# Turning the first expert loop's rows by transposing transfers, with gathers three tiles ahead

## The reference

```python
out = jnp.einsum('teh,te->th', y, combine)           # layer 0: routed experts
sh = jax.nn.gelu(x_flat @ sW1 + sb1, approximate=False)
out = out + sh @ sW2 + sb2                           # and the shared one
...
h = jax.nn.gelu(x_flat @ W1e + b1e, approximate=False)   # layer 1, per expert
y = h @ W2e + b2e
out = acc + ce[:, None] * y
```

## Time and profile before

| | us |
|---|---|
| median of 3 runs | 786.86 (783.21 to 787.51) |
| the profiled execution | 785.51 |
| its span, first to last instruction | 783.7 |
| PE busy | 672.7 (86%) |
| DVE busy | 494.1 (63%) |
| ACT busy | 462.3 (59%) |
| POOL busy | 312.5 (40%) |

### The profile page before, as it was taken

One profiled execution on the slowest core, in us unless ns is written; L12 is line 12 of the kernel. 1 busy time (PEld: TensorE's weight loads), 2 busy tenths in 40 slices (PEclk: granted clock), 3 DMA queues, 4 the chain that ended last, 5 costly groups with the idle time before them and its releaser, 6 DMA issues.

```text
span 783.7 us, 21835 instructions
## 1 busy us (share of the span) xinstructions
PE 672.7 (86%) x7498; PEld 592.1 (76%) x7499; DVE 494.1 (63%) x1227; ACT 462.3 (59%) x1124; POOL 312.5 (40%) x229
## 2 busy tenths in 40 slices
PE   4787899988987899999999936872399999999993
PEld 3454566768877899999989935762399999999993
DVE  4569758696857676777755525967288644544541
ACT  2346667875638786777755615250198766666661
POOL 1100014343562454556555422243235554454442
PEclk9879879999999999999999976955599999999997
DMA  8860100012619633678863339835534454444541
GB/s 263 289 206 28 54 1 1 28 54 71 201 42 317 180 49 53 152 223 246 238 169 46 48 72 409 290 107 116 195 55 79 79 81 72 81 73 68 80 67 22
DMA packets 84451, 96.19 MB, mean 123 GB/s; under 512 B 27419, under 2 KB 70181, under 8 KB 83638
## 3 DMA queue, kind: packets, MB, share of 16 engines
q1 hardware_dynamic: 69334, 74.81, 29.6%
q0 software_dynamic: 15072, 20.84, 16.9%
HBM read 63.73 MB, written 26.79 MB: 115 GB/s over the span
## 4 chain that ended last, share of the span: by engine, by line
PE 66%; DVE 14%; DMA 7%; ACT 4%; issue 4%; POOL 2%; SPq 1%; POOLq 0%; ACTq 0%; DVEq 0%
PE bank L1153 8%; PE bank L1151 8%; PE bank L1152 8%; PE bank L1164 7%; PE bank L1165 7%; PE bank L1166 7%; DMA x_arena<-token_rows,gather_now 3%; DVE weights L1597 2%; DVE ln_stats L1924 2%; PE bank L872 1%; DMA x_sum<-x_arena,add_now 1%; POOL weights L727 1%; PE bank L1043 1%; DVE weights L1691 1%; PE bank L874 1%
## 5 line engine op out<-in xcount | busy, mean ns | idle before, releaser
L1448 ACT ACTIVATE work<-bank,b_cols 128x128 f32<-128x128 f32 x624 | 178.1, 382 | 155.8 <-PE bank L1153 153.0
L1151 PE MATMUL bank<-x_arena,weights 128*128 128x128 f16 x1248 | 217.0, 221 | 11.3 <-DMA x_arena<-x_arena 10.6
L1152 PE MATMUL bank<-x_arena,weights 128*128 128x128 f16 x1248 | 216.9, 221 | 0.0
L1153 PE MATMUL bank<-x_arena,weights 128*128 128x128 f16 x1248 | 216.8, 221 | 0.0
L1849 DVE TENSOR_TENSOR work<-work 128x512 f16<-128x512 f32 x156 | 100.9, 688 | 138.8 <-ACT work L1456 119.4
L1164 PE MATMUL bank<-weights,work 128*128 x624 | 170.1, 273 | 0.0
L1166 PE MATMUL bank<-weights,work 128*128 x624 | 170.1, 273 | 0.0
L1165 PE MATMUL bank<-weights,work 128*128 x624 | 170.1, 273 | 0.0
L1151 PEld LDWEIGHTS bank<-x_arena,weights 128*128 x1248 | 123.5, 99 | 12.2 <-DMA x_arena<-x_arena 10.7
L1152 PEld LDWEIGHTS bank<-x_arena,weights 128*128 x1248 | 123.5, 99 | 0.4
L1153 PEld LDWEIGHTS bank<-x_arena,weights 128*128 x1248 | 123.6, 99 | 0.0
(11 more groups left out here) (214 smaller groups left out, 1207.1 us busy)
## 6 DMA issues: line engine op xcount, KB each, us to landing
weights<-in_L_ffn_W SPq DMA_DIRECT2D x76, 256.0 KB, 7.0
raw<-in_L_ffn_W SPq DMA_DIRECT2D x44, 256.0 KB
split_dram<-row_arena SPq DMA_DIRECT2D x12, 512.0 KB
weights<-split_dram SPq DMA_DIRECT2D x3, 2048.0 KB, 16.7
token_rows<-row_arena SPq DMA_DIRECT2D x2, 2072.0 KB, 10.8
x_arena<-in_x SPq DMA_DIRECT2D x4, 512.0 KB, 6.5
weights<-in_L_ffn_sW SPq DMA_DIRECT2D x8, 256.0 KB, 7.3
x_sum<-x_arena SPq DMA_DIRECT2D x4, 512.0 KB, 3.2
```

The lines of the kernel that those rows point to most:

```text
L1151: nc.tensor.matmul(o, w1_at[f][c][0].block(), hi, start=c == 0, stop=False)
L1152: nc.tensor.matmul(o, w1_at[f][c][0].block(), lo, start=False, stop=False)
L1153: m = nc.tensor.matmul(o, w1_at[f][c][1].block(), hi, start=False, stop=c == DC - 1)
L1448: m = nc.scalar.activation(hid[:, k, f * P:f * P + P], h_ps[k][half][:, g * P:g * P + P], ACT.Gelu, bias=b1_cols[n][:, f, bass.ds(e, 1)], ...
```

## The change

SyncE turns layer 0's rows too, with the same transposing transfer, so `xT_in` gets a semaphore per layer, and TensorE's turns, their PSUM banks and VectorE's copies go. SyncE's list is written anew: units 28..31 as soon as the table of rows is stored, units 24..27 once TensorE has read the router's scratch (`table_done` in place of `routed`; `padding` moves out of that scratch), turn(0, 0), the store of x batch 3, turn(0, 1), `biases`, units 32..35 and two units of layer 1, and then one turn for each tile 2 to 38, with at most one unit of layer 1 loaded and one staged between two turns. The late loads for layer 1 stand behind turn 33. Gathers go out three tiles ahead in both loops: gather 0 before the last shared_low, gathers 1 and 2 ahead of the loop, gather j+3 in body j. VectorE's pick now waits for the transfer.

```diff
-            for b in range(2, B):
-                store_x(0, b, s_added, TB * (b + 1))
-            biases(0)
-            sp.wait_ge(routed, 1)
-            for u in range(24, 28):
-                load_unit(0, u)
+            store_x(0, 2, s_added, 3 * TB)
             sp.wait_ge(rows_stored[0], 16)
             for u in range(28, 32):
                 load_unit(0, u)
+            sp.wait_ge(table_done, 1)
+            for u in range(24, 28):
+                load_unit(0, u)
+            sp.wait_ge(x_stored[0][0], 16)
+            turn(0, 0)
+            store_x(0, 3, s_added, 4 * TB)
+            sp.wait_ge(x_stored[0][1], 16)
+            turn(0, 1)
+            biases(0)
             sp.wait_ge(s_down_done, STEPS)
             for u in range(32, 36):
                 load_unit(0, u)
...
+            for j in range(2, ROUTED):
+                turn(0, j)
+                if j == PRESPLIT_FROM + AHEAD_UNITS[1] + 5:
+                    late_loads()
+                u = j - PRESPLIT_FROM - 3
+                if 0 <= u < AHEAD_UNITS[1]:
+                    split_done(sp, 1, u)
+                    if u + RAW < AHEAD_UNITS[1]:
+                        load_unit(1, u + RAW)
+                    if u >= KEPT:
+                        stage(u)
...
+            def turn(n, j):
+
+                k = j % 2
+                sp.wait_ge(row_in[k][n], 16 * (j // 2 + 1))
+                if j >= 2:
+                    sp.wait_ge(up_done[n], 2 * (j - 1))
+                sp.dma_start_transpose(xT[:, k, :].rearrange("p (i r) -> p i r", r=P), rows_in[:, k, 0:2 * D]).then_inc(xT_in[k][n], 16)
...
-                    if before_end(j, 2):
-                        gather(n, j + 2, k)
+                    if before_end(j, 3):
+                        gather(n, j + 3, 1 - k)
...
+                gather(n, 1, 1)
+                gather(n, 2, 0)
                 tile_loop(pool, n, body)
...
                 def up(j, q, k):
-                    if n == 0:
-                        pe.wait_ge(xT_ready, j + 1)
-                    else:
-                        pe.wait_ge(xT_in[k], 16 * (q + 1))
+                    pe.wait_ge(xT_in[k][n], 16 * (q + 1))
...
-                    if n == 0 and before_end(j, 1):
-                        turn(j + 1, q + (1 if k else 0), 1 - k)
                     up(j, q, k)
...
-                def pick_weight(j, k):
-
+                def pick_weight(j, q, k):
+
+                    dve.wait_ge(xT_in[k][n], 16 * (q + 1))
```

More of the change, by code:

```diff
@@ L214, in build @@
         from_tile = [w[:, 0:TT * (ROUTED + 1)].bitcast(F16).rearrange("p (k t i) -> p k t i", k=2, t=TT) for w in scratch]
-        padding = [w[:, 0:ROUTED + 1] for w in scratch]
+        padding = r_b[:, 0:ROUTED + 1]
         tile_hot = [w[:, 704:704 + TT * (ROUTED + 1)].bitcast(F16).rearrange("p (k t i) -> p k t i", k=2, t=TT) for w in scratch]
@@ L260, in build @@
         few_ps = bank[7][:, 0:FC * 32].rearrange("p (f r) -> p f r", f=FC)
-        xT_ps = [bank[k][:, 0:256].bitcast(F16) for k in range(2)]
         h_ps = [bank[2:4], bank[4:6]]
@@ L330, in build @@
         row_in = [per_layer(f"row_in{k}") for k in range(2)]
-        rowT_done, xT_ready = sem("rowT_done"), sem("xT_ready")
-        xT_in = [sem(f"xT_in{k}") for k in range(2)]
+        xT_in = [per_layer(f"xT_in{k}") for k in range(2)]
         up_done, hi_done = per_layer("up_done"), per_layer("hi_done")
@@ L647, in _, with late_loads @@
                 load_unit(1, u)
[L648 to L661, removed]
+            def late_loads():
+                for k in range(4):
+                    sp.wait_ge(staged[k], 16 * 3)
+                sp.wait_ge(kvm_stored, 32)
+                sp.wait_ge(kvb_stored, 16)
+                sp.dma_start(kvm.rearrange("p b c e -> p (b c e)"), kv_dram).then_inc(late_in, 16)
+                sp.dma_start(kvb.rearrange("p b d -> p (b d)"), kv_bias_dram).then_inc(late_in, 16)
+                sp.dma_start(gamma, a["L1_xattn_ln_gamma"].partition_broadcast(P)).then_inc(late_in, 16)
+                sp.dma_start(beta, a["L1_xattn_ln_beta"].partition_broadcast(P)).then_inc(late_in, 16)
+            for j in range(2, ROUTED):
[9 more added lines that the diff above has]
+                        stage(u)
             sp.wait_ge(added[0], 16 * ROUTED)
@@ L680, in _ @@
                 load_unit(1, u)
[L682 to L688, removed]
             for b in range(2):
@@ L692, in _ @@
             for j in range(ROUTED):
-                turn(j)
+                turn(1, j)
             sp.wait_ge(added[1], 16 * ROUTED)
@@ L741, in first_rows @@
                 gather(n, 0, 0)
-                gather(n, 1, 1)
             def ffn_rows(n):
@@ L764, in body @@
                         add(j - 2, k)
+                gather(n, 1, 1)
+                gather(n, 2, 0)
                 tile_loop(pool, n, body)
-                pool.wait_ge(row_in[1][n], 16 * ((ROUTED + 1) // 2))
+                for k in range(2):
+                    pool.wait_ge(row_in[k][n], 16 * ((ROUTED + 3 - k) // 2))
                 for j in (ROUTED - 2, ROUTED - 1):
@@ L784, in _ @@
                 if m == STEPS - 1:
-                    first_rows(0)
+                    first_row(0)
                 shared_low(m)
@@ L1784, in row_tokens @@
                 V.tensor_scalar(gather_row[:, 0:ROUTED + 1], table, -1.0, 0.0, ALU.add, ALU.max)
-                link(V.tensor_scalar(padding[n], table, 0.0, cst("trash"), ALU.is_equal, ALU.mult))
-                link(V.scalar_tensor_tensor(add_row[:, :], table, -1.0, padding[n], ALU.add, ALU.add))
+                link(V.tensor_scalar(padding, table, 0.0, cst("trash"), ALU.is_equal, ALU.mult))
+                link(V.scalar_tensor_tensor(add_row[:, :], table, -1.0, padding, ALU.add, ALU.add))
             def tile_experts(n):
```

20 lines of the change are left out of this document (4 added, 16 removed).

## The result

The changed kernel takes 797.85 us (median of 4 runs, 795.03 to 798.37), the kernel before 785.08 beside it: ratio 1.0154, 95% interval 1.011 to 1.0197. I had forecast 779, so the sign was wrong. One of e4's four runs, 789.71 us, fell in a slower state of the chip and is left out of its ratio.

The account below looks back on a forecast made before the run. TensorE was taken as the bound: up(2) at 249.7, 36 tiles of 5.30 us and 2.1 us of clock put up(38) at 442.6, 6.9 us earlier. Forecast 779 us, range of 8 in 10 from 771.5 to 786.

Parts of the forecast that it names:

- Term 1: First loop: taking the transposes off TensorE saves 0.22 us a tile, a period of 5.30 us as in loop two.
- Term 2: Before the loop: up(0) waits for gather 0 and a transfer, starting 0.4 us later; cost about nothing, 0 to 2.3.
- Term 3: Loop start: tile 2's transfer queues behind twelve weight loads on SyncE; TensorE stands still 8 us, up(2) at 249.7.
- cheap start: Rival, loop start: turn(0, 2) does not queue behind the loads, up(2) at 244.8, 771.6 us in all; chance 0.15.
- Term 4: Loop start: the lowered clock after TensorE's 8 us idle loses 2.1 us, ends 0 and 2.9.
- Term 5: Rest of the first loop: earlier gathers leave 7.9 us of cover, DMA work 5.0 of 5.3 us; nothing charged.
- "slower" rival: Tiles 15 to 30: transfers land over 7.9 us late behind loads and staging, DMA-bound, 795 us; chance 0.12.

Follow-up runs that it names:

- e4: The kernel before, TensorE's turns kept, with gathers three tiles ahead as the only change: 782.72 us, ratio 0.9880 from three runs.
- e7b: e2 without the twelve staging stores, the second loop's first weights filled from the table of rows instead: 775.51 us, ratio 0.9891.
- e2: The changed kernel with the six units between turns 1 and 2 loaded one behind each of turns 2 to 7: 784.64 us, ratio 0.9947.
- e1: The changed kernel with GpSimd issuing the add before the gather in each body of both loops: 797.79 us, ratio 1.0128.
- e3: The changed kernel with gathers two tiles ahead again, as before, and the transposing transfers kept: 796.79 us, ratio 1.0089.
- e8: e2 with the add before the gather in all tiles but 13 to 29 of the first loop: 786.64 us, ratio 0.9992.
- e9: e2 with staging stores on ScalarE's queue, add before gather except in first-loop tiles 0 to 29, late loads behind the last turn: 778.12 us, ratio 0.9917.
- e13: e9 with the staging stores back on SyncE's queue: 781.32 us, ratio 0.9919.
- e12: e4 with add before gather from tile 30 on and in the second loop, late loads held until up(36) is done: 780.49 us, ratio 0.9903.

## Why the prediction was wrong

**Term 1 (0.22 us a tile) was right.** In tiles 3 to 16 the period is 5.30, and 36 of them follow one another in e7b.

**Term 2 (up(0) 0.4 us later)** measured 1.6: gather 0 landed 5.6 us after its issue, not 4.5. The eight transfers of units 24 to 27 had gone out from 228.9 to 233.1, right up to gather 0 at 233.2, so they were still under way.

**Term 3 (turn(0, 2) behind twelve loads) was right.** Forecast 17.0 us from up(0) to up(2), measured 18.1 and 18.3; the wait 8 us, measured 7.4. Of that, 5.4 us is the landing (7.92 against 2.52), the rest the issues of the loads ahead of it. e2 undid it. The cheap start, my rival for it, is out. One support was weak: the 7.0 us of the earlier trace rows is a median over 76 loads, most of them issued in blocks, and not of a load alone. The Trainium skill ("DMA: Bandwidth & Descriptors", Queues, rings and completion order) has each DMA engine consume the descriptors of one issuing engine's row in ring order; the 7.92 us of that transfer agree with it.

**Term 4 (2.1 us of clock)**: after the wait of 7.37 us the granted clock was 0.64 in 259.48 to 265, and up(2) took 4.7 us in place of 2.85, a loss of 1.9. In size and place right. The clock was low at up(0) too (0.56), but that loss fell into time in which up(2) would have waited for its transfer, and cost nothing.

**Term 5 is the step that failed: "a gather is issued some 0.9 us into up(j-3)" and "I charge nothing, with 7.9 us of cover".** The DMA work came out as I had summed it, 5.0 of 5.3 us (share 0.94 in 340 to 400). The cover was not there.

The gathers did not leave one body earlier. There are still two buffers of rows, so gather j waits for pick j-2, and pick j-2 stands behind a result on VectorE and behind its own transfer. In tiles 20 to 25 of the kernel before a gather went out 5.3 to 5.5 us behind the start of up(j-3); in tiles 10 to 22 of the changed one, but for one tile, it was 4.0 to 4.6, and not 0.9. The issue of gather 12 (302.58, above) and the start of up(9) and the turn of tile 12 that belong to it:

```profile
298.45 0.22 PE L1149 MATMUL bank<-x_arena,weights 128*128 128x128 f16 x1
...
306.67 1.19 SPq L635 DMA_TRANSPOSE x_arena<-x_arena  x1
```

So SyncE wanted the rows 4.1 us after the gather's issue, where I had 7.0. A gather in clear takes 3.6 and just fits; the 6.58 us of a staging tile does not, and the transfer starts late.

Then the waits close cycles. One is gather, transfer, pick, and the gather two tiles later, and must fit into two periods, 10.6 us. In tile 28 it took 13.2: 4.6 from gather to transfer (392.73 to 397.30), 7.3 for the transfer, 1.3 for pick and issue. In tiles 21 to 29 such rounds took 10.5 to 13.6. The other is the chain of adds: the picks of tiles 25 and 26 did not wait for their transfers but for the results ahead of them on VectorE, which waited for adds 20 and 21 to land, 6.8 us for the first. I had given each transfer its own cover, and the cover belongs to the round. e1 and e3 say the same: a cover of 7.9 us would have swallowed a gather that is 2 us late. In e7b, without the staging, the rounds of tiles 18 to 28 took 10.6 each, and no up waits. This was the mechanism of my "slower" rival in half: its place and its tiles were right, its point of decision (a landing 7.9 us late, DMA engines over their capacity) was not. How the 5 us divide between the two cycles is not shown; a third buffer of rows would open the first alone, and I did not run it.

**Term 5 again: "so a tile's time of cover remains" for the add.** I looked at who waits for an add, result j+2, and not at the chain of adds itself, each of which waits for the one before. At 5.2 us a round it has no room in 5.30 to make up a late start, and in the staging tiles its rounds grew to 7.7. In the quiet tiles that costs TensorE nothing. In the staging tiles it holds picks and so gathers, as above. Where the loop ends it costs 5.1 us, and 1.8 in the second loop, for which I had written 0. e1, e3 and e8 brought the first tail back by the order. e9 and e13 have that order only from tile 30 on and kept 15.7 and 16.0: their adds still waited for the one before, with rounds of 5.2 to 5.3, and add 36 was 6.8 and 6.7 us late. With TensorE's turns (e12) the period is 5.52, the adds gained on it from tile to tile, and the tail was 12.0.

In sum from gather 0 on: forecast -6.9; the failed steps add 5.3 (waits of the staging tiles, 198.2 for 192.9), 5.1 and 1.8, terms 2 and 3 2.3 more, and the stretch between the loops was 2.3 shorter, within what it varies. That is +5.3, against 5.2 measured between these two profiles. The profiled runs themselves differ by 12.7; the rest is the 7.4 us ahead of gather 0.

## What to carry to other kernels

Before a latency-bound transfer replaces engine work, write down the whole cycle that its buffers close (gather, transfer, pick, next gather) and compare its length under the heaviest load with as many periods as there are buffers; slack taken transfer by transfer is counted twice. An operation issued "one tile earlier" is no earlier than its buffer comes free: here it was 1 us and not 5.3. On a queue that carries bulk loads, place them one behind each small transfer, not in a block ahead of one (e2: 1.7% for moving six units). When an operation is issued earlier on a shared in-order engine, look at what it now stands in front of, even where that has a tile of room: it may be a chain with no room to catch up, and the bill comes at the end of the loop, or wherever its landing holds something else.

## What the runs showed of the hardware that I had not expected

A transposing transfer of 128 KB took 2.5 us alone and 7.3 to 7.9 us with loads and stores ahead of it on its own queue; a gather 3.6 and 6.6, an accumulating add 3.7 at the end of the loop and 6.8 in the crowd. At a DMA share of 0.94 to 1.00 things that were waited for came late in these runs, and at 0.69 (e7b) none did. The transposing transfer also held SyncE for 1.2 to 1.3 us at its issue, up to 2.3 among loads, where a plain one mostly took 0.4 to 0.6.
